# Two layers of a small transformer on one core: expert slots taken tile by tile, and the first group of the next stage prepared beside them

## What is computed

```python
h = layernorm(x) * (1 + ca) + sa                     # per sequence scale and shift
x = x + ga * attention(h)                            # causal, stage "front"
h = layernorm(x) * (1 + cb) + sb
# expert layer: a router picks 2 of 8 experts for each token
scores = sigmoid(h @ W_router); sel = top2(scores + bias)
shared = (silu(h @ Wg_s) * (h @ Wu_s)) @ Wd_s        # every token
routed = sum over the 2 experts: weight * ((silu(h @ Wg[e]) * (h @ Wu[e])) @ Wd[e])
x = x + gb * (shared + routed)
# time mixing: needs h of the token and of the token before it
h = layernorm(x) * (1 + ca') + sa'
k, v, r = projections of mixes of h[t] and h[t-1]
state = k*v + decay * state;  o = r * (first * k*v + state)   # scan over time
x = x + ga' * (layernorm(o) * g + b) @ Wo
x = x + gb' * channel_mixing(layernorm(x) ...)       # last stage
```

## Time and profile before

| | us |
|---|---|
| median of 3 runs | 1013.38 (1012.75 to 1017.66) |
| profiled execution, its own time | 1010.1 |
| its span in the profile | 1008.3 |
| PE busy | 882.1 (87%) |
| DVE busy | 659.1 (65%) |
| ACT busy | 460.6 (46%) |
| POOL busy | 349.2 (35%) |

### The profile page before, as it was taken

One profiled execution on the slowest core, in us unless ns is written; L12 is line 12 of the kernel. 1 busy time (PEld: TensorE's weight loads), 2 busy tenths in 40 slices (PEclk: granted clock), 3 DMA queues, 4 the chain that ended last, 5 costly groups with the idle time before them and its releaser, 6 DMA issues. The chain is left out here.

```text
span 1008.3 us, 17355 instructions
## 1 busy us (share of the span) xinstructions
PE 882.1 (87%) x5209; PEld 781.8 (78%) x5209; DVE 659.1 (65%) x2013; ACT 460.6 (46%) x1019; POOL 349.2 (35%) x393
## 2 busy tenths in 40 slices
PE   6899999999999488788789999992999999828897
PEld 6789998889998387687679998992788888726676
DVE  4556678455677466665756876774577766647796
ACT  2433443344333476566336754552332222148784
POOL 4612200690000234434414443343856651023331
PEclk9899999899999769878879999997899999968999
DMA  8200000000000223222244433324211100010112
GB/s 277 95 1 1 1 2 1 1 1 1 1 1 1 70 84 116 90 70 91 85 143 122 123 110 105 92 88 126 84 42 43 42 1 1 1 32 1 43 43 83
DMA packets 47833, 58.34 MB, mean 58 GB/s; under 512 B 5631, under 2 KB 42880, under 8 KB 47744
## 3 DMA queue, kind: packets, MB, share of 16 engines
q1 hardware_dynamic: 39888, 39.11, 12.8%
q0 software_dynamic: 6480, 16.92, 4.8%
q10 hardware_dynamic: 1376, 1.20, 0.4%
HBM read 34.91 MB, written 23.22 MB: 58 GB/s over the span
## 5 line engine op out<-in xcount | busy, mean ns | idle before, releaser
L969 POOL DMA_INDIRECT results<-row_tiles,idu x71 | 70.2, 989 | 111.2 <-ACT row_tiles L1076 99.9
L367 ACT CAST pth<-tp 128x512 fp32r<-128x512 f32 (+3 forms) x80 | 41.8, 526 | 128.8 <-PE tp L717 127.2
L953 POOL DMA_INDIRECT region<-row_tiles,posu x64 | 62.0, 969 | 96.4 <-DVE posu L1165 79.3
L547 DVE TENSOR_TENSOR ptl<-tp,pth 128x512 fp32r<-128x512 f32 (+3 forms) x80 | 48.3, 608 | 54.8 <-ACT pth L367 54.7
L80 PE MATMUL cx<-vh,pth 128*128 128x256 f32 x272 | 80.6, 296 | 1.4 <-DVE ptl L547 1.2
L80 PE MATMUL bank<-h3h,weights 128*128 128x512 f32 x192 | 77.8, 405 | 1.4 <-DVE h3l L1618 1.4
L82 PE MATMUL cx<-vh,ptl 128*128 128x256 f32 x272 | 76.8, 282 | 0.0
L81 PE MATMUL cx<-vl,pth 128*128 128x256 f32 x272 | 76.8, 282 | 0.0
L82 PE MATMUL bank<-h3h,weights 128*128 128x512 f32 x192 | 76.8, 400 | 0.0
L81 PE MATMUL bank<-h3l,weights 128*128 128x512 f32 x192 | 76.7, 400 | 0.0
L80 PE MATMUL bank<-big,hh 128*128 (+1 forms) x174 | 71.8, 413 | 0.1
(11 more groups left out here) (368 smaller groups left out, 2753.8 us busy)
## 6 DMA issues: line engine op xcount, KB each, us to landing
row_tiles<-region SPq DMA_DIRECT2D x71, 130.0 KB, 2.1
pairs<-results SPq DMA_DIRECT2D x14, 512.0 KB, 4.8
x<-in_x SPq DMA_DIRECT2D x8, 512.0 KB, 11.0
out<-x SPq DMA_DIRECT2D x8, 512.0 KB, 2.9
early<-in_wmod SPq DMA_DIRECT2D x2, 768.0 KB
early<-in_wmod SPq DMA_DIRECT2D x1, 1536.0 KB
spare<-in_wg SPq DMA_DIRECT2D x8, 192.0 KB
spare<-in_wu SPq DMA_DIRECT2D x8, 192.0 KB
```

The costliest lines, as they stand in the source:

```text
L367: a_.copy(pth[:, m % 2, 0:w], tp[:, m % 2, 0:w]).then_inc(s["pt_hi"], 1)
L547: vec.tensor_tensor(ptl[:, m % 2, 0:w], tp[:, m % 2, 0:w], pth[:, m % 2, 0:w], ALU.subtract).then_inc(s["pt_lo"], 1)
L953: g_.indirect_dma_start(region, bass.IndirectOffsetOnAxis(ap=posu[:, c, t:t + 1], axis=0), hb[:, G % HB, j], None).then_inc(scattered[G % ...
L969: g_.indirect_dma_start(results, bass.IndirectOffsetOnAxis(ap=idu[:, j % 8:j % 8 + 1], axis=0), y[:, j % YR, 0:D], None, bounds_check=KS * ...
```

## The change

What it does, by engine:

- **Slot table.** DVE no longer compares slot numbers with running sums over experts. It marks which (tile, expert) pairs exist (`there`), numbers them by a scan with the tile as the outer index (`order`), and lets partition p find the pair with number p+1 (`mine`, `in_e`, `in_t`). A product with the identity and one matmul with ones bring expert and tile to all partitions (`slots_known`). Slots thus take tile 0 of every expert, then tile 1 of every expert, and so on; all rows of the first 1024 tokens lie in the first 64 slots, those of the first 512 in the first 32.
- **First two groups read early.** SP reads the pairs of group 0 behind the load of slot 44 and those of group 1 behind the last load, each after a wait for the results of slots 0 to 31 or 0 to 63.
- **Group 0 under the slots.** POOL sums, gates and adds the four tiles in 12 instructions, one behind each result write of slots 46 to 57. DVE takes their statistics in its iterations 59 to 61, POOL makes the factors behind the write of slot 62, ACT makes one normalised tile at the end of each of its iterations 64 to 67, and PE turns them in its iteration 71, ahead of the last `down`.
- **Time mixing** starts with `h_of(0)` and `h_lo(0)`; `edge(0)` follows them. `add_bias(0)` now stands ahead of `normalise(1)`, and PE's `turn_z(1)` moves from behind V0 to behind K1 of group 0.
- The shared expert's weights get tensors of their own (`gsh`, `gsl`, `dsh`, `dsl`), over which `pairs_a` and `z3` are laid later; `dec` is computed at the program's start instead of behind the slots; POOL builds a few more constants.

The core of the diff:

```diff
+            a_.activation(k.dec[:], k.cols[:, :, COL["decay"]], ACT.Exp)        # ACT, front
...
+        def normalise(pool, G): ...          # as before, now callable from both phases
+        def z_next(act, G, j):
+            act.wait_ge(u["nmr_set"], G + 1)
+            need(act, u["zt3_done"], G * KC)
+            nc.scalar.activation(z3[:, j], k.x[:, G * GT + j], ACT.Identity, bias=nmr3[:, G % 2, j:j + 1],
+                          scale=rstd3[:, G % 2, j:j + 1]).then_inc(u["z3_done"], 1)
+        def turn_next(pe, G): ...            # the former turn_z
...
+            def load_pairs(G):               # SP
+                for r in range(YR):
+                    sp.wait_ge(y_out[r], 16 * (G + 1) * GT * E // YR)
+                need(sp, u["whole"], G)
+                for c in range(KS):
+                    sp.dma_start(pairs_a[:, c], by_token[:, c, G * GT:(G + 1) * GT]).then_inc(pair_in[0], 16)
             for j in range(SLOTS):
                 load(j)
...
+                if j == 44:
+                    load_pairs(0)
+            load_pairs(1)
...
+                if 46 <= j < 58:             # POOL, behind the result write of slot j
+                    i, step = (j - 46) % GT, (j - 46) // GT
+                    r, xt = pairs_a[:, 0, i], k.x[:, i]
+                    if step == 0:
+                        pool.wait_ge(pair_in[0], 32)
+                        g_.tensor_tensor(r, r, pairs_a[:, 1, i], ALU.add).then_inc(u["first_sum"], 1)
+                    if step == 1:
+                        pool.wait_ge(u["first_sum"], i + 1)
+                        g_.tensor_tensor(r, r, k.gate[:, 2], ALU.mult).then_inc(u["first_gated"], 1)
+                    if step == 2:
+                        pool.wait_ge(u["first_gated"], i + 1)
+                        last = g_.tensor_tensor(xt, xt, r, ALU.add)
+                        if i == GT - 1:
+                            last.then_inc(u["whole"], 1)
+                if j == 62:
+                    normalise(pool, 0)
...
+                if 64 <= j < 64 + GT:        # ACT, behind y_of(j - 2)
+                    z_next(act, 0, j - 64)
...
+                if j in (59, 60):            # DVE, last in its iteration j
+                    v.wait_ge(u["whole"], 1)
+                    for i in (2 * (j - 59), 2 * (j - 59) + 1):
+                        last = vec.bn_stats(bn3[:, i], k.x[:, i])
+                    last.then_inc(u["bn_done"], 1)
+                if j == 61:
+                    v.wait_ge(u["bn_done"], 2)
+                    for i in range(GT):
+                        last = vec.bn_aggr(mv3[:, 0, i], bn3[:, i])
+                    last.then_inc(u["stats"], 1)
...
+                    if j == 2 and G == GROUPS:   # PE, end of the dense phase
+                        pe.wait_ge(s["spread"], 1)
+                        nc.tensor.matmul(lg[:, 0:2 * SLOTS], plain[:], spread.rearrange("p i j -> p (i j)"), start=True,
+                                         stop=True).then_inc(s["slots_known"], 1)
...
+                if j == SLOTS:               # PE, slots
+                    turn_next(pe, 0)
...
+            add_bias(0)                      # POOL, time mixing, after add_pairs(1)
+            normalise(pool, 1)
...
-            act.wait_ge(u["whole0"], 1)      # ACT, time mixing
+            h_of(0)
             edge(0)
-            z_of(0)
-            h_of(0)
...
-                if G + 1 < GROUPS:           # PE, behind V0
-                    turn_z(G + 1)
+                if 0 < G and G + 1 < GROUPS:
+                    turn_next(pe, G + 1)
                 piece(G, 0, R_)
                 piece(G, 1, K_)
+                if G == 0:
+                    turn_next(pe, 1)
```

More of the change, by code:

```diff
@@ L1098, in _ @@
                     a_.copy(woh, wog[:]).then_inc(s["wo_hi"], 1)
-            a_.activation(dec[:], k.cols[:, :, COL["decay"]], ACT.Exp).then_inc(s["dec_set"], 1)
+                if 64 <= j < 64 + GT:
+                    z_next(act, 0, j - 64)
         @block.vector
@@ L1219, in _ @@
                 if G == GROUPS:
-                    c_.link(vec.tensor_tensor_scan(upto[:], plain[:, 0:E], tiles_e[:], 0.0, ALU.mult, ALU.add))
-                    c_.link(vec.tensor_scalar(gone[:], upto[:], -float(USED), None, ALU.add))
+                    flat = lambda a: a.rearrange("p t e -> p (t e)")
+                    c_.link(vec.tensor_tensor_scan(flat(order), plain[:, 0:1].to_broadcast([P, E * TPE]), flat(there), 0.0, ALU.mult, ALU.add))
+                    c_.link(vec.tensor_tensor(order, order, there, ALU.mult))
                 hidden(n + 1)
@@ L1542, in _ @@
                 if G + 2 < GROUPS:
-                    normalise(G + 2)
+                    normalise(pool, G + 2)
             out_rstd(GROUPS - 1)
@@ L1628, in scan @@
                 start = carry[:, c, G - 1:G] if G % GPB else 0.0
-                c3.link(vec.tensor_tensor_scan(st[:], dec[:, c:c + 1].to_broadcast([P, GW]), kv, start, ALU.mult, ALU.add))
+                c3.link(vec.tensor_tensor_scan(st[:], k.dec[:, c:c + 1].to_broadcast([P, GW]), kv, start, ALU.mult, ALU.add))
                 vec.tensor_copy(carry[:, c, G:G + 1], st[:, GW - 1:GW])
@@ L1667, in final @@
                     last.then_inc(u["x3"], 1)
-            for j in range(GT + 1):
-                if j < GT:
-                    v.wait_ge(first_in[j], 16)
-                    r, xt = pairs[:, 0, 0, j], k.x[:, j]
-                    c3.link(vec.tensor_tensor(r, r, pairs[:, 0, 1, j], ALU.add))
-                    c3.link(vec.tensor_tensor(r, r, k.gate[:, 2], ALU.mult))
-                if j:
-                    last = vec.bn_stats(bn3[:, j - 1], k.x[:, j - 1])
-                if j < GT:
-                    c3.link(vec.tensor_tensor(xt, xt, r, ALU.add))
-            last.then_inc(u["bn_done"], 1)
-            v.sem_inc(u["whole0"], 1)
-            v.wait_ge(u["bn_done"], 1)
-            for j in range(GT):
-                last = vec.bn_aggr(mv3[:, 0, j], bn3[:, j])
-            last.then_inc(u["stats"], 1)
-            edge(0)
             for c in range(KC):
                 h_lo(0, c)
+            edge(0)
             stats(1)
-            v.wait_ge(s["dec_set"], 1)
             for G in range(GROUPS):
```

192 lines of the change are left out of this document (99 added, 93 removed).

## The result

| | kernel before | changed kernel |
|---|---|---|
| median of 20 runs, us | 1019.68 (1012.3 to 1025.68) | 1011.27 (1003.08 to 1015.96) |
| profiled execution, us | 1010.1 | 1010.74 |
| its span, us | 1008.3 | 1008.9 |
| PE busy, us | 882.1 | 887.2 |

The ratio is 0.9912, 95% interval 0.9887 to 0.9936: 0.9% faster, about 9 us. The forecast was -9.0 us of 1013.4, also 0.9%. The kernel before came out 6 us slower in this longer series than in the three runs of the prediction, so only the ratio compares: the changed kernel's 1011.27 stands just above the forecast's absolute range (997.5 to 1011.0), but the ratio applied to the 1013.38 that the forecast started from gives 1004.5, against its 1004.4.

The account below looks back on a forecast made before the run. The prediction took PE to bound the slots and the stage behind them, with a 20.1 us PE hole between. Terms -15.7 + 2.0 + 3.0 + 1.7 = -9.0 us took 1013.4 to 1004.4 us, range 997.5 to 1011.0.

Parts of the forecast that it names:

- The sum: Whole kernel: shorter hole, two waits in the slots and one half-clock spell together give -9.0 us.
- The hole: PE's idle stretch between last slot and time mixing: closing it brings `turn_o(0)` 15.7 us earlier.
- in both cases POOL's chain decides, and PE leaves group 1's turning at 704.8: Behind the first 48 projection matmuls: PE, there at 702.8 or later, waits for POOL's tiles of group 1 until 704.8.
- the half-clock spell: At the time mixing's start: a lowered clock needs no charge, since POOL's chain covers that wait.
- The step after it: At `turn_o(0)`: DVE's `gated(0, 1)`, behind `stats(2)`, ends at 715.3, so PE waits 2 us.
- The jump into new code: Behind the last slot: all engines enter the next stage's code with nothing to hide it, taken as 1.0 us.
- The waits in the slots: DVE's wait for POOL's additions costs 2.0 us around slot 61; ACT's wait for the factors costs 3.0 at slot 66.
- The clock: In the slots: half clock behind the 3.0 us wait costs 1.7 us; the shorter wait is not charged.
- The rule of the Trainium skill: A kernel that waits between bursts starts each burst throttled; by it the shorter slot wait costs another 1.7 us.
- the 3.4 us worked out from it: In the slots: half clock charged behind both waits, 1.7 us for the long one and another 1.7 for the shorter.
- What costs nothing: POOL's additions, early reads of pairs, slot table (1 us either way), slot order and moved `dec` add no time.

Follow-up runs that it names:

- run 1: Changed kernel with ACT's and DVE's `edge(0)` moved ahead of `h_of(0)` and `h_lo(0)`; ratio to the kernel before 0.995.
- run 2: Changed kernel with POOL waiting for DVE's `edge(0)` before it sums group 1's pairs, order on ACT and DVE kept; ratio to the kernel before 0.9928.
- run 3: Changed kernel with DVE's statistics of group 0 in iterations 61 and 62 and their aggregation in 63; ratio to the kernel before 0.989.
- run 4: Changed kernel with ACT's four normalised tiles of group 0 in iterations 66 to 69 in place of 64 to 67; ratio to the kernel before 0.9858.
- run 5: Changed kernel with `edge(0)` first, DVE's statistics of group 0 in iterations 61 to 63 and ACT's tiles in 66 to 69; ratio to the kernel before 0.9845.
- run 7: Kernel before with only the new slot table by scan and match, group 0 still read and summed behind the slots; ratio to the kernel before 0.9981.
- run 8: Changed kernel with PE's turning of group 1 back behind V0 of group 0 in place of behind K1; ratio to the kernel before 0.992.

## Why the prediction was right

**The sum** (-9.0): the stages give -8.9, the runs -0.9%. The chains are the right ones; the closeness to 0.1 us is luck. At `turn_o(0)`, where the forecast stopped, the changed kernel was 9.9 us ahead (15.4 less 5.5), and 1.0 of it was lost by the stage's end. The single profiles carry their clock with them: the same slots with the same waits took 180.30, 180.60 and 182.40 us (changed kernel, runs 1 and 2), the same time mixing reached its end at 182.43 to 183.62 (runs 3 and 4). And several terms were wrong and nearly cancelled.

**The hole** (-15.7, measured -15.4). The step "in both cases POOL's chain decides, and PE leaves group 1's turning at 704.8" failed: PE decided there, since POOL's factors came 1.1 us ahead of the forecast, K0 came 0.9 us later, and the half-clock spell, which I had called covered, was paid in full (48 matmuls took 13.94 us, not 11.3). The step after it, `gated(0, 1)` behind POOL's add and `stats(2)`, was right in mechanism; run 1 shows its wait at 1.90 for 2. In the changed kernel it ends 0.24 us ahead of PE's path, which is why the sum held.

**The jump into new code** (1.0): nothing. In its place stands the lock of `edge(0)`, 2.1 us. Had I asked what runs on POOL beside each DVE instruction with two SBUF operands, the row with 129 and 2083 ns would have given it.

**The waits in the slots** (2.0 and 3.0): PE stood idle 1.68 and 3.24 us, and by the turnings they cost 2.65 and 3.67 (runs 3 and 4 take each away alone). The mechanism was right and each size a fifth to a quarter too small. The 0.46 at 653.98 does not belong to the statistics, as I had it ahead of run 3, but stands behind the slow `name`: it is there in run 5 with the statistics moved.

**The clock** (1.7 behind the long wait, none behind the short one): not paid in the profiled execution, but behind seven of the other eight such waits, at 0.6 us for the short one and 1.1 to 2.1 for the long one. The forecast should have been an expectation over both: an estimate from these profiles is four fifths of 0.6 and three fifths of 1.5 (the mean of 1.1, 1.2 and 2.1), 1.4 in all. The rule of the Trainium skill that the prediction cited (a wait between bursts starts the next burst throttled) agrees with seven of the ten waits; the page's own example has waits longer than the shorter one here, so that it covers this one too was my reading. That both count was nearer than my one; the 3.4 us worked out from it was further off than my 1.7.

**What costs nothing**: the table (run 7) and the reads of the pairs, for which no slot waited. Placing the turning behind K1, which the prediction counted inside its chain, is worth 3.8 us at `turn_o(0)` (run 8).

## What to carry to other kernels

Work that is laid under a bound stretch is free only if its first instruction finds its inputs there: two iterations later on an in-order engine took away each of these waits, at 0 to 1.2 us in the last slot. The waits had eaten 5.4 us of the 14.4 that the hole gave. When a hole is closed, the next chains lie close behind: here 2.8 us less hole gave 1.2 or less at the next meeting point and nothing that could be seen at the stage's end, so follow the gain over two or three groups before counting it. And look beside every short DVE instruction with two operands in SBUF for a long GpSimd instruction.

## What the runs showed of the hardware

- A DVE instruction of 128 x 2 elements, both operands in SBUF, took 2.22 us beside a POOL sum of 2.36 us, and 0.13 to 0.16 us without; one with an operand in PSUM was not touched.
- Half clock came behind PE waits of 1.2 to 3.3 us in some executions and not in others, and lasted some 3 to 7 us; idle time of 2.1 us filled with useless matmuls kept the clock up (2 of 2, against 0 of 12 unfilled). What decides it behind one and the same wait stays open.
- The same dense phase took 164.7 to 175.6 us in the kernels with the new table, at granted clocks of 0.83 to 0.76. One profile of a kernel does not measure a change of 1 us outside its own place.
